# A two-stage kernel on one core: first loads held behind a gather, expert outputs in pieces of 128 rows, drain roots ahead of the scatters, last turn written out

## The reference

```
h = attention(emb[x] * 16 + pos)                       # softmax over the query axis
h = h + mixer(layernorm(h))                            # Mamba-2 block: projection, conv of 4 taps, SSD in chunks of 128, gate, output projection
s = softmax(layernorm(h) @ w_router); top 2 of 8 experts, at most 1024 tokens in each
h = h + sum over a token's experts: weight * (gelu(v @ w1[e]) @ w2[e]) + bias
```

## Time and profile before

| | |
|---|---|
| median of 3 runs | 958.42 us (957.29 to 958.70) |
| profiled execution | 958.16 us |
| its span, first to last instruction | 956.4 us |
| mean granted TensorE clock | 0.965 |
| busy shares | PE 93%, DVE 66%, ACT 55%, POOL 53% |
| chain that ended last | PE 81%, DVE 10%, issue 3%, POOL 2%, DMA 2% |

### The profile page before, as it was taken

How to read it: one execution, slowest core, us unless ns; L and a number is a source line. 1 busy time by engine, 2 the same in 40 slices (tenths; PEclk the granted TensorE clock), 3 DMA queues, 4 the chain that set the end, 5 groups by cost and what they waited for, 6 DMA issues and landing times.

```text
span 956.4 us, 17255 instructions
## 1 busy us (share of the span) xinstructions
PE 887.6 (93%) x5580; PEld 785.6 (82%) x5580; DVE 631.6 (66%) x1662; ACT 529.1 (55%) x1094; POOL 505.9 (53%) x503
## 2 busy tenths in 40 slices
PE   5799999999999999999998539999999999999994
PEld 3688888888888888888886429999999999999993
DVE  2477899888988898889887344646363636363631
ACT  1466776677667767776766134545444544444430
POOL 6257776787678767877788311232333232323342
PEclk8799999999999999999998759999999999999998
DMA  8900011001000000000000034343343433332120
GB/s 269 330 26 12 34 46 33 22 33 33 12 22 13 23 13 23 20 16 14 21 22 26 14 103 132 90 88 105 67 109 72 109 72 104 72 105 28 23 61 34
DMA packets 48653, 58.62 MB, mean 61 GB/s; under 512 B 6336, under 2 KB 43819, under 8 KB 48624
## 3 DMA queue, kind: packets, MB, share of 16 engines
q1 hardware_dynamic: 33552, 41.05, 13.1%
q0 software_dynamic: 13632, 17.02, 10.6%
q10 hardware_dynamic: 1440, 0.17, 0.1%
HBM read 34.14 MB, written 29.75 MB: 67 GB/s over the span
## 4 chain that ended last, share of the span: by engine, by line
PE 81%; DVE 10%; issue 3%; POOL 2%; DMA 2%; ACT 1%; DVEq 0%; POOLq 0%; SPq 0%
PE bank L1592 13%; PE bank L1593 13%; PE bank L1594 13%; PE bank L1387 11%; PE bank L1497 5%; PE bank L1332 4%; PE bank L1477 4%; PE bank L1371 3%; PE bank L1346 3%; PE bank L1362 3%; PE bank L1353 3%; PE bank L1449 2%; DVE seg L1051 2%; PE bank L1512 2%; PE bank L1604 2%
## 5 line engine op out<-in xcount | busy, mean ns | idle before, releaser
L637 POOL DMA_INDIRECT out<-ye,tok_slot x56 | 96.7, 1727 | 254.3 <-DMA out<-ye,tok_slot 138.0
L877 ACT ACTIVATE hf<-bank 128x512 f32<-128x512 f32 x128 | 79.5, 621 | 202.4 <-PE bank L1594 201.1
L1264 DVE TENSOR_TENSOR h_lo<-hf,h_hi 128x512 fp32r<-128x512 f32 x128 | 88.6, 693 | 99.9 <-ACT h_hi L879 99.9
L1592 PE MATMUL bank<-w_hi,h_hi 128*128 128x256 f32 x512 | 146.2, 286 | 0.0
L1593 PE MATMUL bank<-w_lo,h_hi 128*128 128x256 f32 x512 | 144.9, 283 | 0.0
L1594 PE MATMUL bank<-w_hi,h_lo 128*128 128x256 f32 x512 | 144.9, 283 | 0.0
L1023 DVE SCALAR_TENSOR_TENSOR xc<-bank,cw,xc 128x253 f32<-128x253 f32 (+2 forms) x288 | 128.2, 469 | 1.7
L1592 PE MATMUL bank<-xe_hi,w_hi 128*128 128x512 f32 x256 | 100.8, 394 | 2.7 <-DVE xe_lo L1256 2.7
L1593 PE MATMUL bank<-xe_lo,w_hi 128*128 128x512 f32 x256 | 100.4, 392 | 0.0
L1594 PE MATMUL bank<-xe_hi,w_lo 128*128 128x512 f32 x256 | 100.2, 391 | 0.0
L585 POOL DMA_INDIRECT slots_dram<-rows,slot x64 | 63.4, 991 | 67.8 <-DVE slot L1152 53.2
(11 more groups left out here) (203 smaller groups left out, 2311.2 us busy)
## 6 DMA issues: line engine op xcount, KB each, us to landing
w_raw<-w SPq DMA_DIRECT2D x16, 1024.0 KB
slots_dram<-zero_row SPq DMA_DIRECT2D x1, 8320.0 KB, 29.7
xe<-slots_dram SPq DMA_DIRECT2D x16, 520.0 KB, 4.4
out<-hb SPq DMA_DIRECT2D x16, 256.0 KB, 2.1
w_raw<-in_wT SPq DMA_DIRECT2D x1, 1288.0 KB, 9.1
slots_dram<-rows,slot POOLq DMA_INDIRECT x64
out<-ye,tok_slot POOLq DMA_INDIRECT x64, 3.7
xg<-emb,idx POOLq DMA_INDIRECT x36, 4.1
```

Source lines behind the costliest of these rows:

```text
L637: g.indirect_dma_start(out, bass.IndirectOffsetOnAxis(ap=tok_slot[q][:, j:j + 1], axis=0), ye[q][:, j, :], None, compute_op=ALU.add).then_ ...
L877: sc.activation(hf[m % 2][:, :], h_bank[i % H_BANKS][:, :], ACT.Gelu_apprx_tanh)\
L1264: vc.tensor_tensor(h_lo[:, m, :], hf[m % 2][:, :], h_hi[:, m, :].bitcast(F32), ALU.subtract)\
L1592: te.matmul(out_, hi, rhi, start=first_, stop=False)
```

## The change

It has five parts. SP waits for the first gather before it loads w_in and w_out, and ACT waits for the same gather ahead of its ten small loads. In stage one the loop ends a turn earlier and turn 8 is written out, without its gathers, and in its second half without the `nf` work; in that half POOL makes `segment_inputs` of chunk 1 straight behind chunk 0, ahead of `with_bias` and `second_root`. In the first half of the drain POOL makes `gated_root` and `second_root` ahead of the four scatters. The first load of stage two is cut into two of 256 rows, with transposes that begin at the first. Expert outputs are weighed, signalled and added a piece of 128 rows at a time, each in a bank's first half, with the weights' low parts ahead of pieces 2 and 3; of the last expert, only pieces 4 to 7 are fetched and written, and pieces 0 to 3 are added.

```diff
     half(1, Turn(1), Turn(1), None, Turn(2))
-    with loop(2, turns + 1) as reg:
+    with loop(2, turns) as reg:
         half(0, Turn(reg), Turn(reg, -1), Turn(reg, -1), Turn(reg))
         half(1, Turn(reg), Turn(reg), Turn(reg, -1), Turn(reg, 1))
+    half(0, Turn(turns), Turn(turns - 1), Turn(turns - 1), Turn(turns), True)
+    half(1, Turn(turns), Turn(turns), Turn(turns - 1), None, True)
     half(0, None, Turn(turns), Turn(turns), None)
...
         ye = [eb(f"ye{q}", [P, JS, DM]) for q in range(2)]
-        base = eb("base", [P, JS, DM])
+        base = eb("base", [P, JS // 2, DM])
         e_now = eb("e_now", [P, 1])
...
         xe_loaded = [dma_signal(f"xe{half_}_loaded", 16) for half_ in range(NG)]
+        first_rows = sem("first_rows")
         slot_info = sem("slot_info")
...
         expert_added = sem("expert_added")
-        H_BANKS, Y0, CHUNKS = 4, 4 * NG, KF
+        H_BANKS, Y0, CHUNKS = 4, 2 * JS, KF
         CHUNK = 2 * KD * FF // CHUNKS
...
         y_bank = bank[1][2:4]
-        LAST_BANKS = (y_bank[0], y_bank[1], x_bank[0], x_bank[1])
...
             sp.dma_start(wv[:, :, :], w_v.rearrange("(k p) n -> p k n", p=P)).then_inc(s_early, 16)
+            sp.wait_ge(gathered[0], gathered.per_turn)
             sp.dma_start(w_in[:, :, :], in_wT.rearrange("(k p) n -> p k n", p=P)).then_inc(s_win, 16)
...
-            for q in range(2):
-                load_slots(q, q)
+            for n, loaded in enumerate((first_rows, xe_loaded[0][0])):
+                sp.dma_start(xe[0][:, 2 * n:2 * n + 2, :],
+                             slots_dram[2 * n * P:2 * n * P + 2 * P, :].rearrange("(j p) c -> p j c", p=P))\
+                    .then_inc(loaded, 16)
+            sp.dma_start(xe[0][:, 4:8, :], slots_dram[GW:2 * GW, :].rearrange("(j p) c -> p j c", p=P))\
+                .then_inc(xe_loaded[1][0], 16)
+            load_slots(1, 1)
             with sp.Fori(1, NE // 2) as r:
...
                     skip_x(b, q, 1)
-                if f:
+                if f and not final:
                     gather_next(f, p)
...
                     describe_rows(t, p)
+                if b and not f:
+                    gated_root(b, q)
+                    second_root(b, q)
+                if t:
                     scatter_rows(t, p)
-                if b:
+                if b and f:
                     gated_root(b, q)
...
                     segment_inputs(f, p, 0)
+                if f and not nf:
+                    segment_inputs(f, p, 1)
                 if t:
...
                     with_bias(t, p)
-                if b:
+                if b and f:
                     second_root(b, q)
-                if f:
+                if f and nf:
                     segment_inputs(f, p, 1)
...
             for p in range(2):
-                pool.wait_ge(gathered[p], gathered.credit * (PAIRS + 1))
+                pool.wait_ge(gathered[p], gathered.credit * PAIRS)
                 pool.wait_ge(scattered[p], 64 * PAIRS)
...
+            def add_rows(n, q, j):
+                hold(pool, ye_ready, n * JS + (2 + j + 1 - JS))
+                g.indirect_dma_start(out, bass.IndirectOffsetOnAxis(ap=tok_slot[q][:, j:j + 1], axis=0),
+                                     ye[q][:, j, :], None, compute_op=ALU.add).then_inc(added, 16)
+                hold(pool, added, n * (16 * JS) + (16 * j + 16 - 16 * JS))
             def add_results(n, q):
                 for j in range(JS):
-                    if j % 2 == 0:
-                        hold(pool, ye_ready, n * (JS // 2) + (2 + j // 2 + 1 - JS // 2))
-                    g.indirect_dma_start(out, bass.IndirectOffsetOnAxis(ap=tok_slot[q][:, j:j + 1], axis=0),
-                                         ye[q][:, j, :], None, compute_op=ALU.add).then_inc(added, 16)
-                    hold(pool, added, n * (16 * JS) + (16 * j + 16 - 16 * JS))
+                    add_rows(n, q, j)
                 pool.sem_inc(expert_added, 1)
...
-                for j in range(JS):
-                    g.indirect_dma_start(base[:, j, :], None, out,
+                for j in range(JS // 2, JS):
+                    g.indirect_dma_start(base[:, j - JS // 2, :], None, out,
                                          bass.IndirectOffsetOnAxis(ap=tok_slot[1][:, j:j + 1], axis=0))\
                         .then_inc(fetched, 16)
+                pool.wait_ge(fetched, 16 * (JS // 2))
...
-                for j in range(JS):
-                    hold(pool, ye_ready, 2 + (NE - 1) * (JS // 2) + (j // 2 + 1 if j < JS // 2 else j + 1 - JS // 4))
+                for j in range(JS // 2):
+                    add_rows(NE, 1, j)
+                for j in range(JS // 2, JS):
+                    hold(pool, ye_ready, 2 + JS * (NE - 1) + j + 1)
                     g.indirect_dma_start(out, bass.IndirectOffsetOnAxis(ap=tok_slot[1][:, j:j + 1], axis=0),
...
             assert len(small) == N_SMALL
+            act.wait_ge(gathered[0], gathered.per_turn)
             for dst, src in small:
...
                     act.wait_ge(w_loaded, n * 32)
-                    act.wait_ge(y_psum, n * (2 * NG))
+                    act.wait_ge(y_psum, n * JS)
                 sc.activation(w_hi[q].rearrange("p w n -> p (w n)")[:, m * CHUNK:(m + 1) * CHUNK],
...
-                def weigh_onto(g):
-                    half = g % NG
-                    if half == 0:
-                        dve.wait_ge(fetched, 16 * JS)
-                    for j in range(4 * half, 4 * half + 4):
-                        if half == 0:
-                            row, at = y_bank[j // 2], (j % 2) * DM
-                            dve.wait_ge(y_psum, Y0 + 4 * NG * (NE // 2 - 1) + 2 * g + j // 2 + 1)
-                        else:
-                            row, at = LAST_BANKS[j - 4], 0
-                            dve.wait_ge(y_psum, Y0 + 4 * NG * (NE // 2 - 1) + 2 * g + j - 4 + 1)
-                        ins = vc.scalar_tensor_tensor(out=ye[1][:, j, :], in0=row[:, at:at + DM],
-                                                      scalar=w_slot[1][:, j:j + 1], in1=base[:, j, :],
-                                                      op0=ALU.mult, op1=ALU.add)
-                        if half or j % 2:
-                            ins.then_inc(ye_ready, 1)
                 def weigh(g):
                     q, half = g // NG, g % NG
-                    for b in range(2):
-                        if half == NG - 1 and not (last and q):
-                            low_weights(r * 2 + q, 1 - q, b, (w1_split, w2_split)[b])
-                        j = 4 * half + 2 * b
-                        dve.wait_ge(y_psum, r * (4 * NG) + (Y0 + 2 * g + b + 1 - 4 * NG))
-                        vc.tensor_tensor(ye[q][:, j:j + 2, :], y_bank[b][:, :].rearrange("p (j d) -> p j d", j=2),
-                                         bc(w_slot[q][:, j:j + 2].unsqueeze(2), [P, 2, DM]), ALU.mult)\
-                            .then_inc(ye_ready, 1)
+                    for n in range(4):
+                        if half == NG - 1 and n >= 2 and not (last and q):
+                            low_weights(r * 2 + q, 1 - q, n - 2, (w1_split, w2_split)[n - 2])
+                        j = 4 * half + n
+                        if last and g == 2 * NG - 1 and n == 0:
+                            dve.wait_ge(fetched, 16 * (JS // 2))
+                        dve.wait_ge(y_psum, r * (2 * JS) + (Y0 + 4 * g + n + 1 - 2 * JS))
+                        if last and g == 2 * NG - 1:
+                            ins = vc.scalar_tensor_tensor(out=ye[q][:, j, :], in0=y_bank[n % 2][:, 0:DM],
+                                                          scalar=w_slot[q][:, j:j + 1], in1=base[:, n, :],
+                                                          op0=ALU.mult, op1=ALU.add)
+                        else:
+                            ins = vc.tensor_scalar(ye[q][:, j, :], y_bank[n % 2][:, 0:DM], w_slot[q][:, j:j + 1], None,
+                                                   ALU.mult)
+                        ins.then_inc(ye_ready, 1)
...
                         split_x(g + 1)
-                    if last and g >= NG:
-                        weigh_onto(g)
-                    else:
-                        weigh(g)
+                    weigh(g)
                     if g + 1 == NG:
...
-                def last_product(g):
+                def second_product(g):
+                    q = g // NG
+                    pe.wait_ge(w2_split, r * 2 + (q - 1))
                     for j in range(4):
-                        if j < 2:
-                            pe.wait_ge(ye_ready, r * (4 * NG) + (2 * g + j + 1 - 4 * NG))
+                        pe.wait_ge(ye_ready, r * (2 * JS) + (4 * g + j + 1 - 2 * JS))
                         for m in range(KF):
...
                             at = slice(m * DM, (m + 1) * DM)
-                            ins = three(LAST_BANKS[j][:, 0:DM], h_hi[:, m, j * P:(j + 1) * P],
```

(32 more changed lines are left out.)

8 lines of the change are left out of this document (4 added, 4 removed).

## The result

The changed kernel takes **965.00 us** in the median of 20 runs (957.69 to 966.05), the kernel before 958.76 us (957.29 to 962.19, 20 runs): a ratio of 1.0051 (95% interval 1.0037 to 1.0064). It is slower by 0.5%, 6.2 us; forecast was no change, 958.9 us, with a range up to 961.8. The profiled execution took 965.32 us with a span of 963.4, against 958.16 and 956.4 before, so 7.2 us of time and 7.0 us of span are to be found. Of the changed kernel, 3 runs at 957.7 to 959.4 us had 0.963, and 17 at 963.3 to 966.1 had 0.954 to 0.961.

A forecast was written before the change was run, and what follows sets the result against it. TensorE, busy 93% of the span, was taken as the bound, so edits pay only where it is not dense. Terms 2.7 + 0.7 + 2.4 - 0.8 - 0.7 - 3.8 = +0.5 gave 958.7, forecast as 958.9 us, range 955.3 to 961.8.

The forecast's parts named there:

- Last turn written out: Stage one's last full turn: chunk 1's segment work ahead of the roots makes TensorE's segment sums later, +2.4 us (0 to +3.0).
- The one wait of over 4 us that I named: Drain: a sign that TensorE would idle over 4 us ahead of its transposes of norm_2's rows.
- The start: First loads: gather lands at 9.3 us, but ACT's ten issues delay the query product to 16.9, +2.7 us.
- The clock's term: Start: after TensorE stands still, the next eight matmuls run at the half clock, +0.7 us (0 to 1.9).
- The cover for POOL's splits: Start: w_in arrives about 3.1 us later, covered by POOL's 2.70 us idle before its norm root, itself 2.7 later.
- The roots first: Drain: with roots ahead of the scatters, DVE's residual waits for the output projection instead, -0.8 us (0 to -0.9).
- First rows: Start of stage two: halving the first load lets TensorE's transposes begin sooner, -0.7 us (-0.3 to -1.2).
- The end: Last expert: POOL's fetch starts at 910.8 and its last store comes sooner, -3.8 us (-2.4 to -6.0).
- The gather lands no sooner: Slower rival, start: gather still lands at 12.1, query product at 19.7, total +3.3, 961.7 us; chance 0.28 with larger clock losses.
- The moved segment work is harmless: Rival, drain: ACT and TensorE have room, so 2.4 falls away, sum -1.9, 956.5 us; chance 0.30 shared by both faster rivals.
- The end gives all it can: Faster rival, last expert: add not held by the low part, end gains 6.0, 955.5 us; chance 0.30 shared by both faster rivals.

The follow-up runs named there:

- e4: Changed kernel with 22 useless matmuls on TensorE in the drain's waits, around the second segment sums: 960.80 us, ratio 1.0016.
- e6: Changed kernel with ACT's wait for the first gather taken out and POOL's old order in the last full half put back, SP's wait kept: 954.95 us, ratio 0.9946.
- e10: Kernel before with only SP waiting for the first gather ahead of w_in and w_out: 958.00 us, ratio 0.9993.
- e15: Kernel before with the last full turn written out and POOL's order not moved: 961.37 us, ratio 1.0020.
- e11: Changed kernel with 28 useless 128x128 products on TensorE at the start, ahead of the wait for wqk: 958.37 us, ratio 1.0007.
- e1: Kernel before with the changed kernel's start alone, SP and ACT both waiting for the first gather: 961.92 us, ratio 1.0034.
- e3: Changed kernel with POOL's old order in the last full half put back, second_root ahead of chunk 1's segment inputs: 957.83 us, ratio 1.0003.
- e9: Kernel before with the last full turn written out and POOL's segment products of chunk 1 moved ahead: 965.33 us, ratio 1.0063.
- e5: Changed kernel with the start of the kernel before, neither SP nor ACT waiting for the gather: 956.52 us, ratio 0.9997.
- e13: Second profile of the kernel of e9 (kernel before, last full turn written out, segment products moved), a single run: 965.36 us.

## Why the prediction was wrong

The time of the profiled execution is accounted for: start +4.57, removed work -0.67, segment sums +2.6, clock in the drain +3.9, the output projection's own length +0.2, roots -0.85, slots +0.25, first rows -0.7, experts +0.2, end -2.3, behind the last store -0.15, together +7.0 of 7.0 us of span. (The removed work is what the shift lost between the norm root of the start and the drain; no row shows it by itself.)

- **The step that failed is "Last turn written out".** Its mechanical part was right: forecast were segment sums 2.4 us later because rows wait for the roots behind chunk 1, the runs show 2.6, and norm_2 is released by nm, 2.2 us after chunk 1 was done at 521.6. (The one wait of over 4 us that I named is in two, 3.43 and 1.64 us, because the second segment sums waited for gm and fell between.) But the step has no term for TensorE's clock: it was put at nothing, without a reason. I had used such a term for the start and not for the drain, where rows 9 already show it: an output projection of 5.27 us. In the profiled run, one of the 17 with the lower clock, it stayed at half through the own chunks up to the output projection, and this costs 3.9 us. The chance of it was in none of the rivals as a mechanism. e4 shows the cost: with the clock held at full in the drain the time is 4.2 us lower, in spite of the useless work. That the move's longer wait causes the low clock is not shown: the clock falls with the order of before too, and stayed low past the own chunks in e6, e10 and e15, which do not move anything. Why 17 of 20 runs of the changed kernel were in the lower group stays open. (The step's own terms give 522.5 for the sums, where it has 522.6.)
- **The start** was right by its landing (9.37, forecast 9.3) and its releaser (16.77, forecast 16.9). The clock's term was mis-sized: 0.7 taken, 1.8 measured (3.78 less 1.99), which was the upper end of its range. e11 confirms the cause: with TensorE busy there the scores take 1.99 us. But the size is one of two here as well: behind waits of 6.38 and 6.41 us in e1 and e3 the scores took 1.99 us, behind 6.71 and 6.92 us in the changed kernel and in e4 3.78. The cover for POOL's splits held (3.40 us idle ahead of the root).
- **The roots first** gave 0.85 (forecast 0.8), and the residual is released by the output projection as named. **First rows**: 3.0 us from issue to transposes, forecast 2.9, and 0.7 gained. (The section that the prediction cites there gives its fit for DMAs issued from POOL's queue; this load is issued from SP's.)
- **The end** gave 2.3, forecast 3.8. The fetch was on time, but not by the working: counted against the barrier's 9.3 it starts at 910.3, forecast 910.8. The first add was not held by the low part beside it (1.54 us at 899.97; I had let it stand still), the second was (2.90 us at 904.36), and the two errors cancel. The four adds behind it took 19.7 us up to the first store instead of 18.4: two of the four steps took 5.5 and 5.0 us, not 4.6, with 3.90 us of idle time ahead of the third add, for which the profile names no releaser, and 3.21 ahead of the store. That last row names DVE, but the result that the store needs came at 943.21; what it still waited for is the completion of the add before it.
- **The rivals.** "The gather lands no sooner" was false by 2.7 us; SP's wait alone brings it forward (e10). That the time came out above the range is not its doing. "The moved segment work is harmless" is nearly true in e9's and e5's profiles, where the clock was back before the own chunks (0.2 and 0.3 us), which the rival did not foresee as a condition; in e11's it costs 2.1. "The end gives all it can" was false, though its reason, that an add under way may run on, held for the first add.
- The changed kernel's own runs with a clock of 0.963, at 957.7 to 959.4, are where I had forecast all of them. The forecast was one of two outcomes, and the rarer. No profile was taken of these three. If their drain was like e9's or e5's, the number is right by luck: the segment sums would have cost 0.2 instead of 2.4 us, while the end gave 1.5 us less than forecast and the start may have cost 1.1 more.

What stays open is why the clock comes back at once in one run of e9's kernel and not in another. The Trainium skill, "TensorE: Matmul & The Clock Gate", part on the clock gate, says that the chip looks at TensorE's activity in windows that run freely against the kernel, so that the point of return varies from run to run. By that, equal work can have a different return. But the page puts the spread at half a microsecond, and e9 and e13 differ by some 20 us, so the measurement goes beyond what the page says. It puts the cost of the ramp under 1% of a span; e9 and e13 differ by 7.5 us, 0.8%, with 1.9 us of it from the start, which is inside that bound and still more than this whole change was forecast to move. Why odds of 6 in 105 become 7 in 12 by writing a turn out (e15) was not settled; that the drain begins some tenths of a microsecond elsewhere relative to such windows is my guess and was not tried.

## What to carry to other kernels

A stretch in which TensorE waits is to be priced twice: the waits themselves, and the work behind them at the half clock until the clock comes back, which here was under 6 us in one run and over 20 in another of the same kernel. Look for the price in the rows of the kernel before: the clock fell in its drain too, behind waits of under 1 us. Where the same kernel shows groups of runs with different granted clocks, one profile is one draw: compare distances between fixed instructions in several profiles, and count the runs of each group before a part of a change is called dear or free. And a gate that holds large loads back should not also hold small issues on a queue whose engine has work behind them: ten issues of half a microsecond made 5.4 us of path out of cover.
